# A 256-column clear on GpSimd between indirect transfers, in a two-layer expert and attention kernel

## The reference, cut to what matters

```python
x = x + 0.5 * ffn(layernorm(x))      # layer 0 of experts
x = x + attn(layernorm(x))           # linear attention, 16 heads, chunks of 128
x = x + 0.5 * ffn(layernorm(x))      # layer 1, the same weights

def ffn(x):                          # 8 experts, one per token
    expert_idx = argmax(x @ Wr.T + br, axis=-1)
    h = relu(einsum('td,efd->etf', x, W1) + b1)      # 128 -> 512
    y = einsum('etf,edf->etd', h, W2) + b2           # 512 -> 128
    return y[expert_idx, arange(4096)]
```

## Time and profile before

| | us |
|---|---|
| median of 3 runs | 519.77 |
| lowest and highest of them | 517.29 and 520.08 |
| the profiled execution | 516.73 |
| its span in the trace | 514.9 |
| PE busy in the span | 369.8 (72%) |
| DVE busy | 326.6 (63%) |
| POOL busy | 243.6 (47%) |
| ACT busy | 190.3 (37%) |

### The profile page before, as it was taken

One profiled execution on the slowest core, in us unless ns is written; L12 is line 12 of the kernel. 1 busy time (PEld: TensorE's weight loads), 2 busy tenths in 40 slices (PEclk: granted clock), 3 DMA queues, 4 the chain that ended last, 5 costly groups with the idle time before them and its releaser, 6 DMA issues. The chain is left out here.

```text
span 514.9 us, 10079 instructions
## 1 busy us (share of the span) xinstructions
PE 369.8 (72%) x2474; PEld 326.2 (63%) x2474; DVE 326.6 (63%) x972; ACT 190.3 (37%) x570; POOL 243.6 (47%) x246
## 2 busy tenths in 40 slices
PE   4484105999999967967969779666499720699983
PEld 2474105999998745646658667555399620599983
DVE  4745002566657389999999998996666700256641
ACT  1160002555555512343544635402365200255540
POOL 1007771455544457637364582657131277245443
PEclk9655556999999979979899897868699975599998
DMA  8993454788886199000000000003566442277840
GB/s 252 364 390 111 147 175 144 225 246 238 231 279 210 42 296 284 1 1 0 1 1 0 1 1 2 0 32 113 182 194 182 139 150 83 79 206 228 243 127 6
DMA packets 55238, 72.17 MB, mean 140 GB/s; under 512 B 6831, under 2 KB 39884, under 8 KB 54928
## 3 DMA queue, kind: packets, MB, share of 16 engines
q1 hardware_dynamic: 46784, 53.95, 35.2%
q0 software_dynamic: 6016, 13.13, 6.9%
q10 hardware_dynamic: 2384, 4.46, 2.3%
HBM read 45.58 MB, written 27.75 MB: 142 GB/s over the span
## 5 line engine op out<-in xcount | busy, mean ns | idle before, releaser
L953 PE MATMUL bank<-slot_xT,w_ring 128*128 128x128 f32 x736 | 103.4, 283 | 14.2 <-issue 8.2
L953 PEld LDWEIGHTS bank<-slot_xT,w_ring 128*128 128x128 f32 x736 | 93.4, 198 | 16.7 <-issue 12.0
L336 POOL DMA_INDIRECT slots_in<-rows,slot_of x64 | 62.4, 975 | 76.8 <-DVE slot_of L695 58.2
L730 DVE TENSOR_SCALAR hT_b<-bank,b_cur 128x128 f32<-128x128 f32 x184 | 56.0, 347 | 45.2 <-PE bank L953 26.7
L1011 PE MATMUL bank<-outer_all,decay_sb 128*128 128x256 f32 x256 | 75.3, 423 | 8.8 <-DVE outer_all L251 4.5
L251 POOL TENSOR_TENSOR outer_all<-qkv 128x512 f32<-128x512 f32 x60 | 63.9, 1100 | 24.6 <-ACT qkv L476 24.6
L346 POOL DMA_INDIRECT out_x<-ring x46 | 44.7, 972 | 64.6 <-DVE ring L737 42.9
L963 PE MATMUL bank<-w_sb,hT_a 128*128 x368 | 59.5, 285 | 18.7 <-DVE ring L737 17.1
L346 POOL DMA_INDIRECT x<-ring x46 | 44.6, 971 | 55.9 <-issue 31.7
L1011 PEld LDWEIGHTS bank<-outer_all,decay_sb 128*128 128x128 f32 x256 | 51.2, 211 | 28.1 <-issue 10.8
L771 DVE TENSOR_REDUCE o_in<-qS 128x64 f32<-128x512 f32 x64 | 68.0, 1073 | 0.0
(11 more groups left out here) (110 smaller groups left out, 491.8 us busy)
## 6 DMA issues: line engine op xcount, KB each, us to landing
w_ring<-in_w1t SPq DMA_DIRECT2D x92, 256.0 KB
slots_in<-fill SPq DMA_DIRECT2D x4, 3128.0 KB, 18.3
ring<-slots_in SPq DMA_DIRECT2D x92, 136.0 KB
rows<-in_x SPq DMA_DIRECT2D x8, 256.0 KB, 6.6
w_sb<-in_w2t ACTq DMA_DIRECT2D x1, 2048.0 KB, 15.3
rows<-x SPq DMA_DIRECT2D x8, 256.0 KB, 4.3
decay_sb<-in_decay ACTq DMA_DIRECT2D x1, 1024.0 KB, 16.6
slots_in<-rows,slot_of POOLq DMA_INDIRECT x64
```

What stands on the lines that cost most here:

```text
L336: pool.indirect_dma_start(slots_in[u], bass.IndirectOffsetOnAxis(ap=slot_of[u][:, t:t + 1], axis=0), row_of(u % GROUPS * GROUP_TILES + t), ...
L730: last = nc.vector.tensor_scalar(hT_b[G % 2][:, f * P:(f + 1) * P], bank_b[:, f * P:(f + 1) * P], b1_cur[G % 2][:, 2 + f:3 + f], 0.0, ALU. ...
L953: last = mm(to[:, f * P:(f + 1) * P], w1_ring[G % W1_BUFS][:, (2 * half + f) * P:(2 * half + f + 1) * P], slot_xT[G % 2][:, :], start=True ...
```

## The change

`pause()` clears a scratch tile of 256 columns in all 128 partitions on GpSimd, lets the clear signal a semaphore of its own, and makes GpSimd wait for it. It is called after every transfer of `sort_rows` in the second groups (u = 1 and 3: 32 calls) and after every transfer of `scatter` (92 calls). Nothing reads the scratch.

```diff
@@ -109,6 +109,7 @@
         fill = sb("fill", [P, ROW])
+        idle = sb("idle", [P, 256])
@@ -188,7 +189,7 @@
-        fill_ready, ids_ready = sem("fill_ready"), sem("ids_ready")
+        fill_ready, ids_ready, paused = sem("fill_ready"), sem("ids_ready"), sem("paused")
@@ -326,6 +327,14 @@
+            def pause():
+
+                pool.memset(idle[:, :], 0.0).then_inc(paused, 1)
+                pauses[0] += 1
+                pool.wait_ge(paused, pauses[0])
+
+            pauses = [0]
+
             def sort_rows(u):
@@ -336,6 +345,8 @@
                         row_of(u % GROUPS * GROUP_TILES + t), None).then_inc(rows_sorted[u], 16)
+                    if u % GROUPS == 1:
+                        pause()
```

## The result

The changed kernel takes 522.91 us (median of 16 runs) against 519.42 for the kernel before (16 runs): ratio 1.0061, 95% interval 1.0031 to 1.009. It is slower, by 3.5 us, where 16.5 were forecast. The profiled execution took 518.73, its span is 516.9; before, 516.73 and 514.9.

What follows compares the result with a forecast made beforehand. It took a stall from GpSimd's unbroken issuing as the bound, with GpSimd the bound after the change. Layer 0's +0.7 and layer 1's +15.8 us gave +16.5: 533.2 profiled, 536 as median, range 512 to 562.

Steps and rivals of the forecast that it cites:

- The place: GpSimd becomes the bound, its transfers at 2.10 us against PE's 1.90 per tile; layer 1's scatters end 15.8 us later.
- Rival B: GpSimd's transfers themselves starve the others, so pauses only stretch the stall: 549 us profiled, 552 beside the median; chance 0.10.
- the stall: Other engines starve while GpSimd issues second sorts unbroken; gaps of 1.1 us end it, PE starting about 18 us earlier.
- Rival A: Clear hides under the transfer, period 1.75 us, below PE's 1.90: 498 us beside the median; chance 0.20 whole or in part.
- x: Time from a transfer's end to the clear's start on GpSimd, 0 to 0.30 us, taken near 0.
- 0.78 stays: From the clear's end to the next transfer on GpSimd, 0.78 us, its own semaphore being no quicker than DVE's.
- P: Period of one GpSimd transfer with its clear and wait, 2.06 to 2.36 us, taken as 2.10 for sorts and scatters.
- 116 periods: 61 in layer 0 and 55 in layer 1, changing the time by 116 P - 227.2 = +16.5 us.
- P below 1.96: The change in time is zero at P = 1.96; below it the changed kernel is faster.
- the bound of layer 0: GpSimd's sort, scatters and outer products, ending at 194.3 us, set layer 0's end: +0.7 us.
- PE's fifth piece: First attention piece in layer 0 needing GpSimd's outer products; began at 193.58 us, its 7.05 us slack forecast as eaten.
- PE in layer 1: PE finishes the first group's tiles at about 429 us, waits until some 443, finishes the other 23 at about 492.

Runs made afterwards that it cites:

- run 5: Changed kernel with the scatters' bounds check on the second sorts' transfers too: 535.49 us, ratio 1.0319 to the kernel before.
- 8: Changed kernel with a clear of 1024 columns in the second sorts, 256 kept in the scatters: 541.23 us, one run.
- 9: Changed kernel without clears in the second sorts, where GpSimd waits for each transfer's landing before the next: 577.6 us, one run.
- run 1: Changed kernel with pauses in the second sorts alone, taken out of the scatters: 510.02 us, ratio 0.982 to the kernel before.
- 2: Changed kernel with pauses in the scatters alone, taken out of the second sorts: 520.99 us, ratio 1.0046 to the kernel before.
- run 11: Changed kernel with one-column clears throughout, behind every second-sort transfer but only every second scatter: 511.11 us, ratio 0.9871 to the kernel before.
- run 6: Changed kernel with a clear of one column instead of 256 in the scatters, sorts kept at 256: 511.18 us, ratio 0.9843 to the kernel before.
- run 10: Changed kernel with scatters pausing only behind every second transfer, one-column clear, sorts kept at 256: 508.08 us, ratio 0.9828 to the kernel before.
- run 7: Changed kernel with the scatters' pause of 256 columns only behind every third transfer: 510.01 us, ratio 0.9848 to the kernel before.

## Why the prediction was right or wrong

**The place was right for layer 1.** It ends with GpSimd alone, and the scatters' period is 2.07 to 2.09 where 2.10 was forecast. Rival B is out: runs 5, 8 and 9 end the stall of layer 0 with longer gaps. The Trainium skill, DMA: Bandwidth & Descriptors, SWDGE vs HWDGE vs iDMA, says that transfers of SP and ACT never touch GpSimd's descriptor path and are immune to one interference with it, DVE locking GpSimd out. That says nothing of what GpSimd's own issuing does to SP, so the prediction took more from it than it holds. Here SP's weight loads at the start of layer 0 stand 9.1 us apart with GpSimd's gap at 0.30 and 1.6 apart (62.71, 64.31) with it at 1.11 in run 5: SP isn't independent of how GpSimd issues. Rival A's mechanism, a clear hidden under the transfer, is out too: x is 0 and the clear's 0.33 stands whole behind the transfer.

**The step that failed is the last of the period's sum**, "0.78 stays", taken from a scatter and applied to the sorts. It holds for transfers with a bounds check. The sorts' have none, and theirs is 0.28: P is 1.57 there. Of the forecast's 116 periods 32 are sorts: 32 x (2.10 - 1.57) = 17.0 us too many, and 84 scatters at 2.08 instead of 2.10 are 1.7 more. 16.5 - 17.0 - 1.7 = -2.2. On GpSimd's row 4 us come back, by the larger leads where sort and scatter meet and three longer waits in layer 1 (421.17, 454.14 and 489.16, 2.5 us together), so its periods give about +2.1. That the trace, too, has +1.9 to +2.0 is in part luck, as layer 0 doesn't end with GpSimd's row. Run 5, with the bounds check on both kinds, came out at 535.49 for a forecast of 536; its layer 1 takes 17.7 us more than before (117.4 against 99.75), where 15.8 were forecast. I had one answer for two kinds of transfer that differ by the check, and at 1.2 us for each 0.01 of P that mattered more than anything else. That P below 1.96 turns the sign was in the text; that it could be so in the sorts alone was not.

**With it fell the bound of layer 0.** The forecast let GpSimd's outer products end at 194.3 and hold PE's fifth piece. With P at 1.57 in the sort they end at 183.11, and PE, which is there at 185.84, sets the end: layer 0 and attention get 8.1 us shorter instead of 0.7 longer. Part of that the forecast left out, DVE's 2.6 us for outer products without GpSimd beside it; and 0.7 lies ahead of the change.

**The two halves don't add up.** Alone the sorts' pauses gain 1.8% and the scatters' cost 0.5%; together they cost 0.6%. By the traces, in us:

| kernel | second sort of layer 0 to that of layer 1 | from there to the last scatter |
|---|---|---|
| before | 349.8 | 99.75 |
| 1, sorts' pauses | 344.1 | 100.3 |
| 2, scatters' pauses | 350.2 | 104.2 |
| after, both | 342.3 | 109.7 |

The sorts' pauses make layer 1's second sort longer, 26.1 instead of 20.2 us up to the first scatter behind it. In run 1 that is hidden, as the scatters end with PE, at 503.25, 1.1 us behind DVE's last tile. With the scatters paused GpSimd ends the layer, and both are paid in full.

**Second, the stall.** I said a gap of 1.1 ends it; that is so (run 5). The real gap in the sorts was 0.61, which takes off less than half of it in layer 0. In layer 1, where GpSimd is the bound, this costs nothing; in layer 0 it costs at most the 2.7 us by which PE came after GpSimd's outer products.

**Third, PE in layer 1.** I let it finish the first group's tiles, but SP's order stops it sooner: the load of tile 23 waits for the sort and the weight loads from tile 20 on stand behind it, so PE rests from 415.7 to 431.00, until the sort has landed, however well GpSimd's gaps let it run. This too is covered by GpSimd's queue.

How far the others starve, by the gap between two transfers of the second sort, with PE's first product in layer 0 and its distance from PE's first transpose:

| gap, us | kernel | PE's first product | after its transpose |
|---|---|---|---|
| 0.30 | before | 83.56 | 21.5 |
| 0.39 | 11 | 83.35 | 21.4 |
| 0.61 | after | 76.16 | 14.8 |
| 0.61 | 1 | 75.32 | 13.2 |
| 1.11 | 5 | 65.95 | 4.2 |
| 1.24 | 8 | 67.77 | 4.7 |
| 1.73 and more | 9 | 65.61 | 3.8 |

This is the start of layer 0. In layer 1, with the pass under way, the same gaps do more. With 0.30 (before) DVE gives no tile from 412.00 to 439.02, to the end of the sort at 428.4 and 10 us beyond; with 0.39 (run 11) one, at 424.44, from 414.35 to the end of the sort at 432.5. With 0.61 (after) it gives six in 15.2 us and with 1.11 (run 5) six in 12.7 us, until SP's order stops them.

**What stays open.** Why a bounds check costs 0.5 us behind a fresh wait, since it costs nothing in an unbroken row; taking the check off the scatters wasn't tried. Whether it is the gap or the rate of transfers that frees the others: a transfer takes 0.97 in all runs, so a longer gap is always a lower rate too, and no run tells them apart. The first transfer of a sort, which has no check, also starts 0.87 us after DVE's signal; whether its distance comes from the other engine or from something ahead of the loop wasn't tried. And what exactly the starved engines lack: ACT stood still with its input ready, so it isn't SP's loads alone. The queues that the profile calls instruction moved no packet from 30 to 85 us before and from 28 to 76 after, and ACT came back at 82.90 and 75.50, so the stall didn't end with a recorded load of code. Beyond that the trace doesn't say what ended it.

## What to carry to other kernels

Price an added wait per kind of instruction: here a bounds check decides whether a transfer is ready 0.28 or 0.77 us behind the wait, and in a queue that is the bound that difference is multiplied by its length. Where a queue of GpSimd's transfers runs unbroken beside other engines' work, put gaps between the transfers: 0.91 us freed the others in the scatters of run 6, 1.11 in the sorts of run 5. Put them only where the others have work and the queue has slack, since each is paid in full where GpSimd ends the stage. And try the halves of a change apart, but don't add them: here the sorts' half alone gave 1.8%, and the scatters' half cost 0.5% alone and some 2.4% on top of the other, where GpSimd had become the bound.

## What the runs showed of the hardware that I had not expected

- The clear starts right at the transfer's end (60.53 after 59.56 + 0.96), and costs 0.33 with 256 columns, 0.12 with one and 0.96 with 1024.
- The lead of an indirect transfer behind GpSimd's own semaphore is 0.28 without and 0.77 with a bounds check; in an unbroken row it is 0.30 with either.
- At the start of layer 0 the relief from a gap isn't in proportion to it: nothing at 0.39, less than half at 0.61, all at 1.11. In layer 1's scatters it is graded: while tiles wait, PE does one tile in 1.9 us with a gap of 0.91 behind each transfer (run 6), in 2.5 with 0.91 and 0.30 in turn (run 10), in 3.2 with a long gap behind every third (run 7), and hardly any without (run 1). Run 7's time is still no better than run 1's, 510.01 against 510.02.
- Waiting for a sort transfer's landing before the next makes gaps of 1.73 to 5.06 us, so, with the 0.3 us of lead taken off, landing takes 1.4 to 4.8 us beside SP's loads, an estimate.
- The same outer products take DVE 2.50 us alone and 5.11 beside GpSimd's, and GpSimd 4.14 against 5.99.
